# Expert stage with a transposed first layer, weights copied one tile ahead, relus dealt to two engines

## The reference

```python
def _L0_ffn_ref(x, Wg, bg, bias, W1, b1, W2, b2):
    logits = jnp.einsum('sbd,de->sbe', x, Wg) + bg + bias
    vals, idx = jax.lax.top_k(logits, 2)
    w = jax.nn.softmax(vals - max(vals))
    cw = jnp.einsum('sbk,sbke->sbe', w, one_hot(idx, 16))
    h = jax.nn.relu(jnp.einsum('sbd,edh->esbh', x, W1) + b1[:, None, None, :])
    y = jnp.einsum('esbh,ehd->esbd', h, W2) + b2[:, None, None, :]
    return jnp.einsum('esbd,sbe->sbd', y, cw)
```

## Time and profile before

| | |
|---|---|
| time, median of 3 runs | 1120.99 us (1120.59 to 1123.28) |
| the profiled execution, its time | 1120.47 us |
| its span | 1118.7 us |
| mean granted TensorE clock | 0.955 |
| PE busy / PEld busy | 995.7 us (89%) / 834.2 us (75%) |
| DVE busy / ACT busy / POOL busy | 832.9 us (74%) / 592.9 us (53%) / 650.5 us (58%) |

### The profile page before, as it was taken

The page is one execution under the profiler, slowest core; times in us unless marked ns, Lnnn a source line. Parts: engine busy times, 40 slices in busy tenths (PEclk is TensorE's granted clock), DMA queues, the critical chain, the costliest instruction groups (busy, mean ns, idle before and its releaser), DMA issues. The chain is left out here.

```text
span 1118.7 us, 40527 instructions
## 1 busy us (share of the span) xinstructions
PE 995.7 (89%) x13498; PEld 834.2 (75%) x13498; DVE 832.9 (74%) x2572; ACT 592.9 (53%) x1415; POOL 650.5 (58%) x1155
## 2 busy tenths in 40 slices
PE   4999999995999998299957999799999999899993
PEld 4778778784787786189947998588888888788882
DVE  1777777777777776655533555689999999899984
ACT  1666666663666665145523554245556556455653
POOL 2333333332777777566764555668777777677656
PEclk9999999997999999689987999799999999999996
DMA  3411222331443320134423554111111111111101
GB/s 76 94 40 41 50 48 55 72 74 38 109 106 96 93 57 24 43 117 149 142 71 112 150 143 131 47 38 37 34 37 38 34 37 38 31 34 39 34 21 32
DMA packets 106902, 74.39 MB, mean 66 GB/s; under 512 B 21360, under 2 KB 98288, under 8 KB 106736
## 3 DMA queue, kind: packets, MB, share of 16 engines
q1 hardware_dynamic: 98544, 55.40, 18.9%
q0 software_dynamic: 8192, 16.79, 5.2%
HBM read 38.60 MB, written 33.55 MB: 64 GB/s over the span
## 5 line engine op out<-in xcount | busy, mean ns | idle before, releaser
L681 ACT ACTIVATE arena<-PS 77x512 f32<-77x512 f32 (+4 forms) x736 | 307.9, 441 | 411.2 <-PE PS L1197 266.8
L1197 PE MATMUL PS<-arena 128*32 128x128 f32 (+5 forms) x9488 | 430.6, 290 | 46.0 <-DVE arena L1166 21.2
L1197 PEld LDWEIGHTS PS<-arena 128*32 128x32 f32 (+4 forms) x9488 | 346.2, 146 | 111.2 <-DVE arena L1166 31.6
L604 POOL DMA_INDIRECT moe_in<-moe_results,slot x128 | 129.1, 1009 | 139.6 <-PE PS L1197 75.4
L1197 PE MATMUL PS<-w,arena 128*128 x960 | 189.8, 316 | 0.4 <-ACT arena L681 0.4
L524 POOL DMA_INDIRECT moe_rows<-arena x128 | 127.4, 996 | 71.8 <-POOL arena L520 50.3
L539 POOL TENSOR_TENSOR arena<-arena,minus_half 128x2 f32<-128x2 f32 (+1 forms) x70 | 47.6, 680 | 182.7 <-DVE arena L855 164.1
L1197 PEld LDWEIGHTS PS<-w,arena 128*128 128x128 f32 x960 | 135.7, 195 | 13.6 <-issue 1.8
L1078 DVE TENSOR_TENSOR arena<-PS,b_rows 128x256 f32<-128x256 f32 x160 | 67.9, 425 | 83.4 <-PE PS L1197 80.8
L1197 PEld LDWEIGHTS PS<-arena,wk_wq 128*128 128x128 f32 x512 | 79.9, 196 | 44.8 <-issue 42.2
L1090 DVE TENSOR_REDUCE arena<-PS 128x8 f32<-128x616 f32 x128 | 96.4, 795 | 12.8 <-PE PS L1197 10.4
(11 more groups left out here) (149 smaller groups left out, 1671.2 us busy)
## 6 DMA issues: line engine op xcount, KB each, us to landing
moe_rows<-zeros SPq DMA_DIRECT2D x64, 160.0 KB, 2.5
arena<-moe_rows SPq DMA_DIRECT2D x40, 256.0 KB
moe_results<-arena SPq DMA_DIRECT2D x40, 256.0 KB, 2.4
residual<-in_x SPq DMA_DIRECT2D x64, 64.0 KB
w<-in_W SPq DMA_DIRECT2D x32, 128.0 KB
arena<-in_ctxC SPq DMA_DIRECT2D x64, 64.0 KB
out<-arena SPq DMA_DIRECT2D x64, 64.0 KB, 1.6
arena<-in_ctxT SPq DMA_DIRECT2D x32, 77.0 KB, 2.0
```

Of the source, the lines that this page charges most:

```text
L604: g.indirect_dma_start(out=gathered(b, k), out_offset=None, in_=ys_flat[b // CB][:, :], in_offset=bass.IndirectOffsetOnAxis(ap=POS[k][:, b ...
L681: A.activation(o, i, ACT.Copy).then_inc(s[done], 1)
L1197: return T.matmul(o, l, r, start=start, stop=stop)
```

## The change

W1 and b1 are laid out anew in memory: for each expert 256 columns of W1 and two columns with b1 (hidden units on the partitions). Then, in stage B:

- The first layer is computed transposed: the weights are the stationary operand and the transposed input the moving one, as two products of 128 columns (into banks 2/3 and 4/5). The result has hidden units on the partitions, so the two transposes of the hidden tile are gone, and so is the addition of b1 along rows.
[...]
- b1 is now the bias column of the relu. ScalarE does the relu of the first half for all tiles and of the second half for odd tiles; VectorE does the second half for even tiles.
- Lags: input transposition 0, weight copy 1, first layer and relu 2, second layer and b2 4 (instead of 0, 2, 4, 6). The semaphores of these steps are new, and on the steps there are no waits left out in the middle of the loop (`wait_free` in place of `wait_edge`).
- SP issues three weight transfers for an expert in place of four.

```diff
@@ buffers @@
-        hb = [cb(EH) for _ in range(2)]
+        w1t = [cb(WS) for _ in range(2)]
@@ ScalarE @@
+            def hidden(b, p, q, done):
+                A.activation(hT[p][:, q * P:(q + 1) * P], PS[:, 2 + 2 * q + p, 0:P], ACT.Relu,
+                             bias=w1t[p][:, EH + q:EH + q + 1]).then_inc(s[done], 1)
             def step_b(t):
-                if (b := t.at(4)) is not None:
-                    p = t.par(4)
+                if (b := t.at(2)) is not None:
+                    p = t.par(2)
                     act.wait_ge(s["hT_mm"], b + 1)
-                    wait_edge(act, t, s["y_mm"], b - 1)
-                    A.activation(hT[p], PS[:, 4 + p, 0:EH], ACT.Relu).then_inc(s["hT_cp"], 1)
+                    wait_free(act, s["y_mm"], b - 1)
+                    hidden(b, p, 0, "hT0_made")
+                    if p == 1:
+                        hidden(b, p, 1, "hT1_odd")
@@ VectorE @@
-                if (b := t.at(2)) is not None:
-                    p = t.par(2)
-                    e = experts.of(t, 2)
-                    dve.wait_ge(s["h_mm"], b + 1)
-                    wait_edge(dve, t, s["hT_mm"], b - 1)
-                    V.tensor_tensor(hb[p], PS[:, 2 + p, 0:EH],
-                                    b1s[:, bass.ds(e, 1), :].rearrange("q o h -> q (o h)"), ALU.add).then_inc(s["h_made"], 1)
+                if (b := t.at(1)) is not None:
+                    p = t.par(1)
+                    e = experts.of(t, 1)
+                    wait_free(dve, s["hT_mm"], b - 1)
+                    wait_free(dve, s["hT0_made"], b - 1)
+                    if p == 1:
+                        wait_free(dve, s["hT1_odd"], b // 2)
+                    else:
+                        wait_free(dve, s["hT1_even"], b // 2)
+                    V.tensor_copy(w1t[p], W1s[:, bass.ds(e, 1), :].rearrange("q o h -> q (o h)")).then_inc(s["w1t_made"], 1)
+                if (b := t.at(2)) is not None and t.par(2) == 0:
+                    dve.wait_ge(s["hT_mm"], b + 1)
+                    wait_free(dve, s["y_mm"], b - 1)
+                    dve.wait_ge(s["w1t_made"], b + 1)
+                    V.tensor_scalar(hT[0][:, P:2 * P], PS[:, 4, 0:P], w1t[0][:, EH + 1:EH + 2], 0.0,
+                                    ALU.add, ALU.max).then_inc(s["hT1_even"], 1)
@@ TensorE @@
-                if (b := t.at(6)) is not None:
+                if (b := t.at(4)) is not None:
...
-                    pe.wait_ge(s["hT_cp"], b + 1)
+                    pe.wait_ge(s["hT0_made"], b + 1)
+                    pe.wait_ge(s["hT1_odd" if p else "hT1_even"], b // 2 + 1)
...
-                if (b := t.at(4)) is not None:
...
-                    for q in range(2):
-                        last = T.transpose(PS[:, 4 + p, q * P:(q + 1) * P], hb[p][:, q * P:(q + 1) * P], ident[:, :])
-                    last.then_inc(s["hT_mm"], 1)
                 if (b := t.at(2)) is not None:
...
                     pe.wait_ge(s["xsT_cp"], b + 1)
-                    wait_edge(pe, t, s["h_made"], b - 1)
-                    mm(PS[:, 2 + p, 0:EH], xsT[p], W1s[:, bass.ds(e, 1), :].rearrange("q o h -> q (o h)")).then_inc(s["h_mm"], 1)
+                    pe.wait_ge(s["w1t_made"], b + 1)
+                    wait_free(pe, s["hT0_made"], b - 1)
+                    wait_free(pe, s["hT1_odd" if p else "hT1_even"], b // 2)
+                    for q in range(HQ):
+                        last = mm(PS[:, 2 + 2 * q + p, 0:P], w1t[p][:, q * P:(q + 1) * P], xsT[p])
+                    last.then_inc(s["hT_mm"], 1)
```

More of the change, by code:

```diff
@@ L95, in flamingo_two_layers @@
     H1, DH1 = 16, D // 16
-    NE, EH = a["b1"].shape
+    NE, EH, _ = a["W2"].shape
+    HQ = EH // P
+    WS = EH + HQ
     EPS = 1e-5
@@ L117, in flamingo_two_layers @@
     LOOP0 = 16
-    LAST_LAG_A, LAST_LAG_B, LAST_LAG_C = 7, 6, 17
+    LAST_LAG_A, LAST_LAG_B, LAST_LAG_C = 7, 4, 17
     LOOPB = 32
@@ L1053, in _ @@
             assert chain["kq_step"] == SETUP_STEPS
-            dve.wait_ge(s["moe_loaded"], 4 * 16 * NE)
+            dve.wait_ge(s["moe_loaded"], 3 * 16 * NE)
             dve.wait_ge(s["ro_done"], NCH)
@@ L1061, in step_b @@
             def step_b(t):
-                if (b := t.at(6)) is not None:
-                    p = t.par(6)
-                    e = experts.of(t, 6)
+                if (b := t.at(4)) is not None:
+                    p = t.par(4)
+                    e = experts.of(t, 4)
                     dve.wait_ge(s["y_mm"], b + 1)
-                    k = t.ring(6, 2 * GT)
+                    k = t.ring(4, 2 * GT)
                     if k % GT == 0:
@@ L1306, in _ @@
             pe.wait_ge(s["kq_step"], 2)
-            pe.wait_ge(s["moe_loaded"], 4 * 16 * NE)
+            pe.wait_ge(s["moe_loaded"], 3 * 16 * NE)
             for last in ("OT0_cp", "KA_cp", "xT1_cp", "V0_cp", "x1_made", "xT2_cp", "lg_made"):
@@ L1462 @@
                                    np.zeros_like(data["ctxT"][:, :, :full - nk])], axis=2)
+    w1, b1 = data.pop("W1"), data.pop("b1")
+    ne, _, eh = w1.shape
+    data["W1b"] = np.concatenate([w1.transpose(1, 0, 2), b1.reshape(ne, eh // 128, 128).transpose(2, 0, 1)], axis=2)
     nc = bacc.Bacc("TRN2", target_bir_lowering=False, num_devices=1)
```

16 lines of the change are left out of this document (4 added, 12 removed).

## The result

The changed kernel takes **1132.23 us** (median of 4 runs, 1131.88 to 1132.65), the kernel before 1121.83 us in the same comparison (4 runs): a ratio of 1.0096, 95% interval 1.008 to 1.0111. The forecast was 1125.5 us, slower, in a range of 1113 to 1134. So the sign and the range hold and the size does not: +4.9 us were worked out from the profile, +10.4 us were measured. The profiled execution took 1132.65 us, with a span of 1130.8 us against 1118.7.

The account below looks back on a forecast made before the run. TensorE bounds each chunk and GpSimd's scatters the wait between; afterwards handovers bind. Chunk 1 +5.0, low clock -1.0, drain -0.9 and scatters +1.8 give +4.9 on 1120.47 us; forecast 1125.5 us, range 1113 to 1134.

Parts of the forecast that it names:

- only chunk 1 pays: Stage B: tile time counts in chunk 1 alone until chunk 0 has used up its 19.9 us wait for scatters.
- TensorE's own instructions, 1.00 us a tile: Stage B after the change: y 0.44, h 0.44, input 0.11 make 1.00 us a tile, against 1.207 before.
- Copy, 0.29: VectorE's weight copy over 128 partitions' tile weights in stage B: length taken as 0.226 + 0.07 = 0.29 us.
- Chain B: Stage B, odd steps without a table load: h, ScalarE's two relus, TensorE's waits and registers; 2.29 us for two steps.
- Chain A: Stage B, the step in four with VectorE's table load: y, b2 addition, load, weight copy, h; 2.86 us for two steps.
- I take 1.27: Stage B tile time after the change, between 1.29 from the chains and 1.24 from their cheap ends; 1.207 before.
- The ramp at the low clock: The 5.8 us at the lower clock in stage B: 3.0 us extra before, 2.0 after, so -1.0 us.
- The drain: From the last input tile to the last b2 addition: 5.75 us before, 4.8 after, so -0.9 us.
- The scatters: Chunk 1: about 60 of 64 GpSimd transfers run beside VectorE's copies, 0.03 us longer each, so +1.8 us.
- the rival built on it: GpSimd is held: each of 60 transfers waits half a copy, +8.7 in place of +1.8, 1132.4 us; chance 0.08.
- The second one: Copy takes 0.43 us, one column a cycle, and the word 0.48: 1.33 to 1.35 a tile, 1131.6 us; chance 0.14.
- The rival with a free word load: VectorE's table load costs nothing as its sequencer runs ahead: 1.15 us a tile, 1114.6 us; chance 0.15.

Follow-up runs that it names:

- e7: Changed kernel with four weight buffers, copy two steps ahead, four relu buffers, second layer at lag six, VectorE's and TensorE's table words loaded early: 1109.3 us, 0.9894 of the kernel before.
- e8: Kernel before, with VectorE loading each word of the expert table twice: 1129.7 us, 1.0076 of the kernel before.
- e6_word_twice: Changed kernel, with VectorE loading each word of the expert table twice: 1175.2 us, 1.0361 of the kernel before.
- c_before: Kernel before, unchanged, measured again in the second job: 1137.6 us.
- c_after: Changed kernel, unchanged, measured again in the second job: 1149.2 us, 1.0119 of the kernel before.
- job 3: Third measuring job, with four follow-up kernels (e7, e8, e9, e10); the kernel before took 1122.1 us in it.
- e10: Changed kernel, with VectorE loading one expert table word once for all tiles, so wrong experts' weights are used: 1118.4 us, 0.9967 of the kernel before.
- e9: Changed kernel, with ScalarE computing all relus, also the second half of even tiles, and VectorE none: 1130.1 us, 1.0080 of the kernel before.
- e1: Changed kernel, with VectorE loading each next table word two steps before first use, behind the previous step's weight copy: 1142.9 us, 1.0054 of the kernel before.
- e2: Changed kernel with four weight buffers instead of two and the weight copy two steps ahead of TensorE instead of one: 1143.9 us, 1.0063 of the kernel before.
- e5_both_word: Changed kernel with four weight buffers, copy two steps ahead, four relu buffers, second layer at lag six, VectorE's table word loaded early: 1134.4 us, 0.9981 of the kernel before.
- e3_y_late: Changed kernel with four relu buffers instead of two, second layer and b2 addition at lag six instead of four: 1147.4 us, 1.0095 of the kernel before.

## Why the prediction was right in sign and short by half

**What bounds the kernel before, and that only chunk 1 pays: right.** Chunk 0 took 11.0 us longer (108.5 against 97.5) and the time did not show it; e7 shows the other side.

**TensorE's own instructions, 1.00 us a tile: right.** The third gap of the changed kernel is 1.00, three of four in e7.

**Copy, 0.29: right** (0.297). **Chain B, 2.29: right** (2.30 in the median, from the y of one such step to the y two steps on).

**Chain A, 2.86: this is the step that failed.** From y to y it is 3.07 us in the median, 3.15 in the round shown. Its terms, as medians over 17 rounds of chunk 1:

| from y (step with the load) | in the sum | measured |
|---|---|---|
| to the start of the table load | 0.78 | 0.78 |
| table load | 0.40 | 0.62 |
| end of the load to the start of the copy | 0.59 | 0.60 |
| start of the copy to the y two steps on | 1.09 | 1.03 |

The term that was mis-sized is the load, by 0.2 us on every fourth tile; all others stand within 0.06. The rounds themselves show it: with the fixed terms at 2.41, the round with a load of 0.74 us (642.0) takes 3.15 and the one with 0.31 us (669.1) takes 2.76. I took the 0.94 of one step of the earlier trace rows for the load's price, and the load in that step had 0.40, although gave the spread, 299 to 710 ns, and one step is one draw from it. And in a chain with no slack the whole of the load counts, where the kernel before showed none of its one load (e8). The 0.07 for a second wait came out, but the row it was read from does not show it: the addition at 522.20 stood behind VectorE's own pass, which ended at 522.15.

**"I take 1.27": a second, smaller slip.** My own chains gave 1.29, and I leaned to their cheap ends. Measured: 1.348 in the mean of chunk 1, (3.07 + 2.32) / 4, which lies above the forecast's own 1.23 to 1.32; that the time still fell into 1113 to 1134 is the room of the range. So 79 steps cost +11.0 us where the sum had +5.0. The sum's last line has a slip too: 1120.47 + 4.9 and 0.5 for the median give 1125.9, not 1125.5; the rivals were worked out from 1120.99.

**The smaller terms.** The ramp at the low clock gives 1.9 back (107.5 is 1.0 above 79 x 1.348; before it was 2.9 above) where I had 1.0. The drain gives 0.9, as forecast. The scatters cost 0.6 at most, where I had 1.8: 954/978/1472 ns against 954/974/1469. The rule of the Trainium skill ("SBUF — State Buffer", section "SBUF: two separate sides"), by which such a copy keeps GpSimd from writing the descriptors of its transfers, does not show in the length of the transfers beside the 160 copies; the rival built on it falls. (The row that I took for agreement, stands beside a pass with two inputs and not beside such a copy.) It was the copy that got longer: 16 of the 160 took more than 0.33 us, up to 0.54, and each of the 16 overlapped one of GpSimd's indirect transfers. One is in the round shown (`641.41 0.45 DVE L1087`, beside a transfer of 0.94 us from 640.81), and its gap of 1.41 us is above the median of 1.25. In chunk 1 there are 5 such copies, so the time hardly shows them. Nor did the clock fall inside the chunks; with the longer waits of e6_word_twice it did (1.57 us a tile).

**Stage A, +2.6 us in the profiled execution: not forecast, and not of the change.** Stage B began at 479.5 and 479.4 us in c_before and c_after, and at 474.5, 475.0, 476.3 and 476.5 us in the four kernels of job 3. It is in the 12.1 us of the spans and for the most part not in the 10.4 of the medians. In the after trace it arises between 257 and 297 us, where TensorE comes back after the route of chunk 0 with the clock low. The granted clock stands at 0.50 there for 13.7 us in the traces that reach stage B at 474.5 (before, e10) and 475.0 us (e8), and for 17.1 us in those that reach it at 476.3 to 477.1 us (changed kernel, e7, e9). What makes it the one or the other was not tested.

**The rivals.** The second one's number (1.33 to 1.35 a tile, 1131.6 us) is the time measured, but half of its cause is wrong: the copy is not 0.43 long. It had the word at 0.48, too short, and the copy too long, and the sum came out, by luck. The rival with a free word load gave 1.15 us a tile and 1114.6 us; e10 comes near it, with 1.14 from the medians and 1118.4 us.

**What I said would show it.** Unequal steps with TensorE idle ahead of h after a table load: yes. First load of chunk 1 at 590.6 to 594: yes, 593.52. End of chunk 0 at about 578: no, 585.6. "TensorE's waits for VectorE's copy" do not appear under that name: the profile puts them down to ScalarE's L679, which in the round shown had ended 1.8 us before the copy did.

## What to carry to other kernels

A load of a register from a table is work of the queue, not of the engine: it is in no busy time, it stands between whatever instructions the queue has around it, and here moving it helped only where it left every chain, not where it went to another place between two results that are each needed one step later (e1, e2). When a change takes slack out of an order (lags of 2 become 1), price each queue instruction at its median or above, over many rounds and not from one. And two chains that alternate have to be relaxed together: a deeper buffer for one alone took 4.4 or 4.2 us off chunk 1, for both 15.9, and with the loads of both queues moved the change became a gain, 12.7 us against the kernel before.

## What the runs showed of the hardware

**Late releases.** In the first two jobs all kernels were slower, the kernel before by 15 us, with the engines' own durations unchanged. What differs is the time from the record of the matmul that makes a result to the start of the instruction that waited for it, where the waiter was idle. Counted in stage B:

| | waits | median, longest (us) | over 0.6 us |
|---|---|---|---|
| changed kernel, first trace: h to ScalarE's relu | 160 | 0.31, 0.46 | none |
| c_after, the same | 137 | 0.31, 1.41 | 20 |
| before, first trace: transposes to ScalarE | 318 | 0.31, 0.51 | none |
| c_before, the same | 167 | 0.31, 1.38 | 44 |
| e8_before_twice (job 3), the same | 319 | 0.31, 0.51 | none |

In the waits of TensorE in chunk 1 they show as "issue", with more of them and longer ones (engine, line, releaser: us in total, times, longest); first the changed kernel, 608 to 700 us, then c_after, the same stretch:

```profile
PEld PS L1212 <- issue: 7.1, 29, 0.4
...
PE PS L1212 <- issue: 0.2, 1, 0.2
```

```profile
PEld PS L1212 <- issue: 12.3, 36, 1.0
...
PE PS L1212 <- issue: 4.9, 12, 0.9
ACT arena L739 <- issue: 4.8, 5, 1.3
```

A kernel bound by one engine hides part of this and one bound by handovers does not: chunk 1 grew by 2.3 us before (98.4 to 100.6) and by 4.8 us after (107.5 to 112.3), and the ratio went from 1.0096 to 1.0119. In the 44 late cases of c_before the record of the semaphore's update is itself late, and ScalarE starts 0.02 to 0.04 us behind it, so the waiter is not what is slow. Whether the matmul or its signal is late can't be told, since the profile models the matmuls' ends, and what causes it was not found. It does not go with the chip's number alone: the record has chip 7 for the first job and for the third, 3 for the second.

**The same table load takes 0.3 us or 0.6.** TensorE's takes 302 ns in the median everywhere. VectorE's takes 606 ns behind the b2 addition (a pass out of PSUM) in the changed kernel, and 309 behind the weight copy in e5_both_word. The instruction ahead is not the reason: in e2_copy_ahead and e3_y_late the load stands behind the same b2 addition, and the kernel before has it both ways. In this order, e5_both_word, e2_copy_ahead, e3_y_late, c_before; the first trace of the kernel before has 476:

```profile
L68 DVEq TENSOR_LOAD <-tile_experts x39: 298/309/512, 484.3 to 689.3; - x39
```

```profile
L78 DVEq TENSOR_LOAD <-tile_experts x40: 299/305/857, 483.2 to 704.3; - x40
```

```profile
L78 DVEq TENSOR_LOAD <-tile_experts x40: 300/303/554, 483.4 to 706.0; - x40
```

```profile
L78 DVEq TENSOR_LOAD <-tile_experts x40: 299/310/652, 482.6 to 698.1; - x40
```

What the traces do show is that a load without transfers beside it is short. I took all of VectorE's loads in stage B, except the first and e10's, and the busy share of the DMA engines in the first 0.3 us of each. Where the share was under 0.1, 142 of 145 loads took less than 0.35 us; where it was 0.9 or more, 73 of 208, and in the changed kernel 32 of 39 loads stand there. That is not the whole cause: in e3_y_late 11 such loads were all short. No run changes the transfers alone, so the cause stays open, and with it how much of the gains of e1 to e3 over c_after (a median of 412 ns) comes from their shorter loads.

The Trainium skill ("DMA: Bandwidth & Descriptors", section "Latency and other measured facts") gives a floor of about 600 ns for such a load; here the shortest took 295 ns on TensorE's queue and 298 on VectorE's, with the table in SBUF, and the measurement decides.
